# A twelve-sublayer decoder on one core: quantised weights made inside the four-key-head attention, unrolled loops, and the inner tile scaled on ScalarE

## The reference, cut to what matters

```python
# l1f: mixture of experts; 16 experts of inner size 176, 4 per token, capacity 128, plus a shared expert of 352
gact = silu(einsum('ech,ehi->eci', xg, w_gate))
mid  = gact * einsum('ech,ehi->eci', xg, w_up)
eout = einsum('eci,eih->ech', mid, w_down) * wbuf[..., None]
# l2x: attention to ctx with its 54 highest scores kept (clip_k = 54)
scores = coef * einsum('bsd,bnd->bsn', Q, ctx)
scores = scores - max(scores)
thr = top_k(scores, 54)[0][..., -1:]
scores = where(scores < thr, -inf, scores)
out = einsum('bsn,bnd->bsd', softmax(scores), ctx) @ W_o.T
# l2f: gated MLP, inner 704, weights and activations rounded to 8-bit steps by row
s(v)  = max(max|v| / 127, 1e-8);  q(v) = round(v / s(v)) * s(v)
gate, up = split(q(x) @ q(w_gate_up).T)
out = q(silu(gate) * up) @ q(w_down).T
# l3f: MLP, inner 1024; activations in 8-bit steps, weights rounded to -1, 0, 1 times their mean absolute value
out = bitlinear(gelu(bitlinear(x, w1)), w2)
```

## Time and profile before

| | us |
|---|---|
| median of three executions | 2930.05 (2928.51 to 2932.92) |
| the profiled execution, its own time | 2934.89 |
| its span | 2933.1 |
| busy: PE / DVE / ACT / POOL | 2248.4 / 1900.4 / 1283.9 / 353.7 |
| granted TensorE clock, mean | 0.882 |

### The profile page before, as it was taken

The page is one execution under the profiler, slowest core; times in us unless marked ns, Lnnn a source line. Parts: engine busy times, 40 slices in busy tenths (PEclk is TensorE's granted clock), DMA queues, the critical chain, the costliest instruction groups (busy, mean ns, idle before and its releaser), DMA issues. The chain is left out here.

```text
span 2933.1 us, 45191 instructions
## 1 busy us (share of the span) xinstructions
PE 2248.4 (77%) x18630; PEld 1725.2 (59%) x18679; DVE 1900.4 (65%) x3121; ACT 1283.9 (44%) x1627; POOL 353.7 (12%) x161
## 2 busy tenths in 40 slices
PE   7975278999999999997138789999953457877643
PEld 4654146777777767777124579999933224554422
DVE  5765677778887788875882434334437785773676
ACT  4642155666666666664422133333321343443144
POOL 0000012222232222320115000000000011000000
PEclk9987689999999999998569899999986679997867
DMA  3000121122121221222125400000000000000000
GB/s 131 1 1 12 23 64 49 54 75 55 49 54 56 73 55 50 53 60 72 61 82 146 166 23 0 0 0 0 0 8 1 30 0 24 2 1 15 1 29 29
DMA packets 159610, 117.72 MB, mean 40 GB/s; under 512 B 116176, under 2 KB 146000, under 8 KB 153680
## 3 DMA queue, kind: packets, MB, share of 16 engines
q1 hardware_dynamic: 156368, 110.99, 12.3%
q0 software_dynamic: 3072, 4.33, 0.9%
HBM read 97.64 MB, written 17.64 MB: 39 GB/s over the span
## 5 line engine op out<-in xcount | busy, mean ns | idle before, releaser
L1447 DVE SCALAR_TENSOR_TENSOR ctx_chan<-l1a_raw,l1a_cw,ctx_chan 128x1024 f32<-128x1024 f32 x192 | 230.8, 1275 | 19.5 <-ACT ctx_chan L1298 18.5
L1060 PE MATMUL banks<-x_chan,l1a_wp 128*128 128x512 f32 x512 | 230.6, 604 | 5.0 <-DMA l1a_wp<-in_l1a_wp_dram 5.0
L1024 POOL TENSOR_TENSOR l1a_sq<-ctx_chan 128x1024 f32<-128x1024 f32 x16 | 152.3, 9517 | 356.7 <-ACT ctx_chan L1302 356.7
L1060 PEld LDWEIGHTS banks<-x_chan,l1a_wp 128*128 128x128 f32 x512 | 98.1, 194 | 116.9 <-issue 110.8
L2475 PE MATMUL banks<-x_chan,l2a_wq 128*128 (+1 forms) x1024 | 124.2, 282 | 9.5 <-ACT l2a_ready L2378 4.9
L2475 PEld LDWEIGHTS banks<-x_chan,l2a_wq 128*128 128x128 f32 x1024 | 122.6, 198 | 11.4 <-issue 5.6
L1097 PE MATMUL banks<-l1a_wo,l1a_oT 128*128 128x256 f32 x512 | 121.8, 387 | 0.0
L1045 POOL TENSOR_TENSOR l1a_al<-l1a_aT,l1a_outer 128x1024 f32<-128x1024 f32 x32 | 74.8, 2359 | 327.2 <-DVE l1a_aT L1507 327.2
L2496 PE MATMUL banks<-l2a_wo,l2a_oT 128*128 128x256 f32 x512 | 113.2, 379 | 1.2 <-ACT l2a_oT L2402 1.2
L96 PE MATMUL banks<-ident,x_tok 128*128 128x128 f32 x288 | 56.8, 360 | 74.5 <-DVE x_tok L134 58.5
L1068 PE MATMUL banks<-l1a_wz,x_chan 128*128 128x256 f32 x512 | 113.7, 380 | 0.0
(11 more groups left out here) (604 smaller groups left out, 5908.2 us busy)
## 6 DMA issues: line engine op xcount, KB each, us to landing
ctx_tok<-l1a_rows_mem SPq DMA_DIRECT2D x16, 1024.0 KB, 6.6
l1a_sq<-l1a_norm_mem SPq DMA_DIRECT2D x16, 1024.0 KB, 4.5
ctx_tok<-in_ctx_dram SPq DMA_DIRECT2D x3, 2048.0 KB, 12.4
ctx_chan<-in_ctxT_dram SPq DMA_DIRECT2D x3, 2048.0 KB, 15.8
l1f_wgu<-in_l1f_wgu_dram SPq DMA_DIRECT2D x4, 1408.0 KB, 10.7
moe_sums<-l1x_zero SPq DMA_DIRECT2D x2, 2176.0 KB, 11.0
l1a_wp<-in_l1a_wp_dram SPq DMA_DIRECT2D x8, 512.0 KB, 3.3
l1f_wgu<-moe_sums SPq DMA_DIRECT2D x8, 512.0 KB, 8.1
```

The lines of the kernel that those rows point to most:

```text
L1024: P.tensor_tensor(sq[:, 0, :], conv[:, 0, :], conv[:, 0, :], ALU.mult).then_inc(s["k_squared"], 1)
L1060: mm = MM(ps[:, 2 * (u % 2) + q, :], wp[:, c, u * 128:(u + 1) * 128], g.xT[:, c, t0:t0 + 512], start=c == 0, stop=c == 1)
L1447: V.scalar_tensor_tensor(t, raw[:, u, :, j:j + S], cw[:, c, j:j + 1], t, ALU.mult, ALU.add).then_inc(s["conv_done" if step == 2 else "conv ...
```

## The change

- **l1a, l1x, l1f.** `l1f_wd0` is laid out in one piece on the host and loaded during l1x into `g.mem`, so l1f's SP queue issues only `wgu` and `wd1`, in another order, and its third and fourth batch wait for the last gather. The fourth piece of the shared expert is made ahead of the experts, and DVE's work at the end is in another order. `ctx` is no longer loaded back there.
- **l2a.** DVE's loop is unrolled. After each of the tiles 1 to 12 DVE does one of twelve weight tasks: for each of the four matrices of l2f and l3f the scales, the division, the rounding. SP loads the matrices and their transposes (made on the host) into `g.mem`, writes the scales to DRAM and reads them back spread over all partitions, and at the end loads `ctx` back.
- **l2x.** Queries, scores and the scaling of scores (now on ACT) go by quads of tiles; the selection, the mask and sum (one instruction), the normalising (now on ACT) and all that follows go by groups of 4, 4, 4, 2 and 2 tiles. PE adds `x` by a product with the identity, and ACT moves the sum to `x`. Layer norm is split, 14 tiles and 2.
- **l2f, l3f.** The weights are there already. `x` is quantised by quads. The loop goes tile by tile, unrolled, and the up-projection runs three tiles ahead. The inner tile is scaled with the constant on ACT, for all tiles in l2f and for the odd ones in l3f. The statistics of layer norm are taken in the loop; layer norm is split, 12 and 4.
- **The output** is stored in four pieces inside l3f, as tiles are done.

```diff
 # l1f, SP
             for n in range(4):
+                if n == 2:
+                    sp.wait_ge(fetched[RING - 1], 16)
                 sp.dma_start(wgu[:, e]..., d["l1f_wgu"][n]).then_inc(w_loaded[n], 16)
-                sp.dma_start(wd0[:, e, :]..., d["l1f_wd0"][n]).then_inc(w_loaded[n], 16)
...
 # l1f, PE
             shared_in(2)
+            shared_in(3)
...
 # l2a, DVE
-            tiles(v, step)
+            for i in range(B):
+                step(i, i == 0, i == B - 1)
+                if 1 <= i <= 3 * len(matrices):
+                    (weight_scales, weight_divided, weight_rounded)[(i - 1) % 3]((i - 1) // 3)
...
 # l2x, DVE
+    GROUPS = ((0, 4), (4, 8), (8, 12), (12, 14), (14, 16))
...
+            def select(n):
+                t0, t1 = GROUPS[n]
+                v.wait_ge(s["sc_out"], (t1 + GROUP - 1) // GROUP)
...
+                v.wait_ge(s["exped"], n + 1)
+                for t in range(t0, t1):
...
+                    ins = V.scalar_tensor_tensor(probs[:, t, :], sc[:, t, :], best[:, t, at:at + 1], probs[:, t, :], ALU.is_ge, ALU.mult, accum_out=rsum[:, t:t + 1])
...
+            for n in range(len(GROUPS)):
+                select(n)
+                if n:
+                    stats(*GROUPS[n - 1])
+                if n == len(GROUPS) - 1:
+                    moments(0, EARLY)
+                    normalise(0, EARLY, 1)
...
 # l2f, l3f
+        def act_scales(i):
+            return not ternary or i % 2 == 1
...
+            # SP, the last sublayer alone
+                for t0, t1 in ((0, 4), (4, 8), (8, 12), (12, 16)):
+                    sp.wait_ge(s["ln_out"], t1)
+                    sp.dma_start(g.out[t0:t1].rearrange("b s d -> s b d"), g.x[:, t0:t1, :]).then_inc(s["stored"], 16)
...
+            # ACT
+                if act_scales(i):
+                    act.wait_ge(s["h_inverse"], i + 1)
+                    A(h[t][:], h[t][:], ACT.Identity, bias=toround[:, 0:1], scale=rh[t][:, 0:1]).then_inc(s["scaled_act"], 1)
...
+                if i + 2 < B:
+                    curved(i + 2)
...
+            # DVE
+            for q in range(QUADS):
+                quad(q)
             scale_up(0)
+            scale_up(1)
+            for i in range(B):
+                scale_inner(i)
+                if i + 2 < B:
+                    scale_up(i + 2)
+                if i >= 1:
+                    scale_down(i - 1)
+                if i >= 2:
+                    stats(i - 2)
...
+            invert(0, EARLY, 1)
+            normalise(0, GROUP)
+            scale_down(B - 1)
...
-        store_out(nc, g, out)
```

More of the change, by code:

```diff
@@ L2335, in layer2_attention @@
         SHARE = HEADS // KV
+        staged = g.mem[:].rearrange("p b d -> p (b d)")
+        inverse = L.sb("inverse", [128, 1408])
+        scales = L.sb("scales", [128, 2, 11])
+        matrices = [(wt, part, (wt.up, D)[part - 1], (D, wt.inner)[part - 1]) for wt in g.quantised for part in (1, 2)]
         block = L.block()
@@ new lines, in queries_moved, with scores_moved @@
+            def queries_moved(q):
+                for m in range(DC):
+                    act.wait_ge(s["queries"], q * DC + m + 1)
+                    A(qT[:, m, q * 512:(q + 1) * 512], ps[:, (q * DC + m) % 2, :], ACT.Copy).then_inc(s["q_out"], 1)
+            def scores_moved(q):
+                act.wait_ge(s["scores"], q + 1)
+                if q == 0:
+                    act.wait_ge(s["coef_made"], 1)
+                A(sc[:, q * GROUP:(q + 1) * GROUP, :].rearrange("p t n -> p (t n)"), ps[:, 2 + q % 2, :], ACT.Identity, scale=coef[:, 0:1]).then_inc(s["sc_out"], 1)
@@ new lines, in _ @@
+            act.wait_ge(s["knobs_loaded"], 16)
+            A(ex[:, 2:3], knobs[:, 2:3], ACT.Exp, scale=-1.0).then_inc(s["knobs_exp"], 1)
+            A(ex[:, 3:4], knobs[:, 3:4], ACT.Exp).then_inc(s["knobs_exp"], 1)
+            for q in range(QUADS):
+                queries_moved(q)
+                scores_moved(q)
+                if q == 1:
+                    exps(0)
+            for n in range(len(GROUPS)):
+                normed(n)
+                if n < len(GROUPS) - 1:
+                    exps(n + 1)
+                else:
+                    A(g.scratch[:], g.ones[:, 0:1], ACT.Sqrt)
+                    act.wait_ge(s["ln_var"], 1)
+                    A(g.rstd[:, 0:EARLY], g.rstd[:, 0:EARLY], ACT.Sqrt).then_inc(s["ln_sqrt"], 1)
+                attended(n)
@@ new lines, in normalise @@
+            def normalise(t0, t1, part):
+                v.wait_ge(s["ln_sqrt"], part)
+                link(V.reciprocal(g.rstd[:, t0:t1], g.rstd[:, t0:t1]))
+                for t in range(t0, t1):
+                    V.tensor_scalar(g.x[:, t, :], g.x[:, t, :], g.moments[:, t, 0:1], g.rstd[:, t:t + 1],
+                                    ALU.subtract, ALU.mult).then_inc(s["ln_out"], 1)
+            for n in range(len(GROUPS)):
+                select(n)
[4 more added lines that the diff above has]
+                    normalise(0, EARLY, 1)
@@ new lines, in _, with __init__, sb @@
+            stats(*GROUPS[-1])
+            moments(EARLY, B)
+            normalise(EARLY, B, 2)
+class Quantised:
+    def __init__(self, nc, ctx, name, inner, halves):
+        self.name, self.inner, self.up, self.ternary = name, inner, inner * halves, halves == 1
+        self.chunks = [min(128, inner - k) for k in range(0, inner, 128)]
+        def sb(part, shape, dt=F32):
+            return ctx.enter_context(nc.sbuf_tensor(f"{name}_{part}", shape, dt))
+        self.q1T = sb("q1T", [128, DC, self.up], BF16)
+        self.q2T = sb("q2T", [128, len(self.chunks), D], BF16)
+        self.row1 = sb("row1", [128, self.up])
+        self.row2 = sb("row2", [128, D])
+        self.spread = [nc.dram_tensor(f"{name}_spread{n}", (2, m), F32, kind="Internal").ap() for n, m in ((1, self.up), (2, D))]
@@ L2717, in quantised_ffn @@
+def quantised_ffn(nc, g, wt):
+    ternary, inner, UP, W2 = wt.ternary, wt.inner, wt.up, wt.chunks
+    C2 = len(W2)
+    whole = inner // 128
+    QUADS = B // GROUP
+    EARLY = 12
+    with Layer(nc, wt.name) as L:
         sx = L.sb("sx", [128, B])
@@ L2780, in _ @@
+            for i in range(B):
+                pool.wait_ge(s["back_made"], i + 1)
+                P.tensor_tensor(g.x[:, i, :], g.x[:, i, :], back[i % 2][:], ALU.add).then_inc(s["added"], 1)
         @block.tensor
         def _(pe):
-            pe.wait_ge(s["diag_made"], 1)
-            for n in range(0, NB, 4):
-                k = min(4, NB - n)
-                mm = nc.tensor.matmul(g.ps[:, n // 4, 0:k * 128], g.ones[:], diag[:, n:n + k, :].rearrange("p k n -> p (k n)"), start=True, stop=True)
@@ new lines, in scale_down, with stats, moments @@
+            def scale_down(i):
+                v.wait_ge(s["down"], i + 1)
+                if i >= 2:
+                    v.wait_ge(s["added"], i - 1)
+                V.scalar_tensor_tensor(back[i % 2][:], down_bank[i % 2], sh[i % 2][:, 0:1], wt.row2[:], ALU.mult, ALU.mult).then_inc(s["back_made"], 1)
+            def stats(t):
+                dve_stats(v, g, t, (s["added"], t + 1), s["ln_stats"])
+            def moments(t0, t1):
+                for t in range(t0, t1):
+                    v.wait_ge(s["ln_stats"], t + 1)
+                    V.bn_aggr(g.moments[:, t, :], g.stats[:, t, :]).then_inc(s["ln_mean"], 1)
+                v.wait_ge(s["ln_mean"], t1)
+                V.tensor_scalar(g.rstd[:, t0:t1], g.moments[:, t0:t1, 1], 1e-5, None, ALU.add).then_inc(s["ln_var"], 1)
@@ new lines, in invert, with normalise @@
+            def invert(t0, t1, part):
+                v.wait_ge(s["ln_sqrt"], part)
+                link(V.reciprocal(g.rstd[:, t0:t1], g.rstd[:, t0:t1]))
+            def normalise(t0, t1):
+                for t in range(t0, t1):
+                    V.tensor_scalar(g.x[:, t, :], g.x[:, t, :], g.moments[:, t, 0:1], g.rstd[:, t:t + 1],
+                                    ALU.subtract, ALU.mult).then_inc(s["ln_out"], 1)
+            for q in range(QUADS):
+                quad(q)
+            scale_up(0)
@@ L2941 @@
+            stats(B - 1)
+            moments(EARLY, B)
+            invert(EARLY, B, 2)
+            normalise(EARLY, B)
 RH = 2
```

612 lines of the change are left out of this document (320 added, 292 removed).

## The result

| | before | after |
|---|---|---|
| median, us (4 executions each) | 2930.44 (2928.51 to 2932.92) | 2798.26 (2791.89 to 2801.91) |
| ratio, 95% interval | | 0.9546 (0.9525 to 0.9567) |
| the profiled execution, its own time and span | 2934.89, 2933.1 | 2791.89, 2790.0 |

The account below looks back on a forecast made before the run. PE was taken to set l2a, DVE and the handovers to it l2f and l3f. Stage gains 11 + 0 + 33 + 39 + 45 = 128 us take the profiled 2934.9 to 2806.9, by the median 2802; range 2780 to 2836.

Parts of the forecast that it names:

- The sum: Gains of l1f, l2a, l2x, l2f and l3f add up, as stages meet at barriers: 11 + 0 + 33 + 39 + 45 = 128 us.
- l1f, 11: l1f: gathers freed of weight loads 5.4 us, shared piece moved 3.4, tiles normalised early about 2; sum 11, bounds 5 to 14.
- l2a, 0: l2a: twelve weight tasks fit in DVE's 10.24 us of waiting for PE per tile; gain 0, range -1 to +6 us.
- Rival C: l2a: weight tasks stop DVE and so PE, making the kernel slower; decides from 21 us a task; 2979 us at 25; chance 0.02.
- l2x, 33: l2x: selection starts at the first quad's scores; stage ends at 2246.1 against 2279.1, gain 33 us (19 to 37).
- rival A: l2x and both loops: handovers set the pace, short bursts run PE at 1.2 GHz; gain 85, time 2845 us; chance 0.17.
- l2f and l3f, start: Starts of l2f and l3f: first inverse after 18.7 instead of 43.65 us and 18.4 instead of 42.4; gains 25 and 24.
- l2f, loop: l2f's loop: 4.6 us a tile on DVE plus 0.2 of stalls, 78 instead of 83.1 us; gain 5.2, bounds -8 to 8.
- l3f, loop: l3f's loop: 4.0 us a tile plus 0.5 of stalls, 74 instead of 82.4 us; gain 8.4, bounds -7 to 16.
- Ends: After the last scaling back: l2f's end 8.9 instead of 17.9 us, gain 9; l3f's end with store 10.3, gain 12.7.
- Rival B: l2x, l1f and both loops: DVE alone sets the pace, no stalls; l2x gains 37, total 145, time 2785 us; chance 0.14.
- D: Starts of l2f and l3f: x's quantising and PE's turns hide what was removed; starts give 12, not 49; 2839 us; chance 0.03.

Follow-up runs that it names:

- reordered start: Changed kernel with ACT loading the curve's table and applying the curve to tile 0, and DVE scaling up tile 0, before the fourth quad: 2793.25 us, ratio 0.9546.

## Why the prediction was right, point by point

- **The sum.** 128 forecast, 128.1 measured over the five stages. That close it is luck: l2x is 4 under, l2f 4 over. The further 15 us of the two profiles lie in the seven other stages and are scatter; between the medians the gain is 132.2. The two largest gains, 44 us in the starts of l2f and l3f and 37 in l2x, are read from the places where the two timelines part; no run puts the old starts or the selection over 16 tiles back.
- **l1f, 11 for 10.3.** The experts' end gains 5.5 (forecast 5.4). The piece gives 3.3 at the end (3.4). DVE's new order there gives 3.8 after the last shared output, but PE now waits 2.2 us for it to free the sums: 1.6 where 2 was put. That the piece lies in a wait was only half true: it delays the first turn by 1.8. The 7.5 us that the prediction took for a load of 2 MB are those of a store; the load in l1x landed in 8.8 us and cost nothing there.
- **l2a, 0 for 0.** Right, with more room than was claimed. Rival C's rule, 21 us a task before it turns the sign, was not reached even with three tasks and a DMA wait in one tile.
- **l2x, 33 for 36.7, and 31 to 37 over nine profiles.** First selection at 12.5 us for 13.1; from there to the last inverse 68.1 for 68.6. The end, 13.5 forecast, is 10.8 in one clock level and 13.3 to 14.7 with the other in it. This is rival A's mechanism, and it is real in l2x, but priced too high there: it takes 2.5 to 4 us at the end and up to 2 before it, not 13.
- **l2f and l3f, start, 25 and 24 for 22.2 and 21.9.** The step that failed is "ACT's and PE's part for the first quad lies under DVE's other quads; uncovered it would cost 2 to 3". The first quad was covered. Uncovered were the curve's table and the last quads, since ACT handles all four before the first curve, and DVE waited 4.73 and 5.16 us for that. The reordered start shows it, 4.2 and 4.8 us sooner. That the first inverses came only 2.8 and 2.1 us after the forecast's 18.7 and 18.4 has two more reasons: DVE's four quads took 11.4 us, not 13.0, and the terms written down for l2f add up to 17.7, not 18.7 (l3f's figure follows from it).
- **l2f, loop, 5.2 for 3.9.** The pitch of a tile was 4.88 us, and 4.93 to 4.97 in the others, for 4.8. The mis-sized term is DVE's product, 0.95 in the earlier trace rows and 1.20 on average now, for a reason told below. That alone is 3.8 us in 15 tiles, and the loop missed by 1.2, so the other terms were together 2.6 us too high.
- **l3f, loop, 8.4 for 11.2.** The stall of 0.5 a tile was too much; the pitch is 4.29.
- **Ends, 9 and 12.7 for 9.1 and 12.6.** Right.
- **Rival B** had l2x's 37 right and its reason wrong for l3f, where DVE's work can grow by 5.6 us with no change. **A**'s pitches of 5.7 and 5.5 us did not come (4.88 and 4.29). **D** was wrong: the starts gave 44 us.
